# A linear-attention layer whose outputs are made feature first, with the key-value sums as weights and the denominators repeated per column

## The reference

```python
def _kernel_features(x, random_matrix):
    x_proj = jnp.einsum('bhsd,dm->bhsm', x, random_matrix)
    return (jax.nn.elu(x_proj) + 1.0) * INV_SQRT_M
...
q_prime = _kernel_features(q, random_matrix)      # 16 heads x 32 features
k_prime = _kernel_features(k, random_matrix)
kv = jnp.einsum('bhsm,bhsd->bhmd', k_prime, v)    # 32 x 8 per head
k_sum = k_prime.sum(axis=2)
out = jnp.einsum('bhsm,bhmd->bhsd', q_prime, kv)
normalizer = jnp.einsum('bhsm,bhm->bhs', q_prime, k_sum)[..., None]
normalizer = jnp.maximum(normalizer, 1e-06)
out = out / normalizer
out = out.transpose(0, 2, 1, 3).reshape(B, S, D)
return out @ Wo + bo
```

## Time and profile before

| | |
|---|---|
| median of three runs | 478.55 us (477.23 to 478.70) |
| the profiled execution | 478.46 us |
| its span, first to last instruction | 476.4 us |
| PE busy | 440.1 us, 92% |
| DVE busy | 374.5 us, 79% |
| ACT busy | 233.6 us, 49% |
| POOL busy | 104.9 us, 22% |
| granted TensorE clock, mean | 0.982 of 2.4 GHz |

### The profile page before, as it was taken

The page is one execution under the profiler, slowest core; times in us unless marked ns, Lnnn a source line. Parts: engine busy times, 40 slices in busy tenths (PEclk is TensorE's granted clock), DMA queues, the critical chain, the costliest instruction groups (busy, mean ns, idle before and its releaser), DMA issues. The chain is left out here.

```text
span 476.4 us, 8304 instructions
## 1 busy us (share of the span) xinstructions
PE 440.1 (92%) x3049; PEld 223.3 (47%) x3085; DVE 374.5 (79%) x1000; ACT 233.6 (49%) x324; POOL 104.9 (22%) x103
## 2 busy tenths in 40 slices
PE   8789979999999999999799999998999999998783
PEld 3333323333432334333243456665766675675772
DVE  6299887889689888987986298869786897887466
ACT  2405646666676665675468612336335623634220
POOL 9891070800637000200002000210020022003012
PEclk9999989999999999999999999999999999999788
DMA  5765433122432024331003222321122112000001
GB/s 160 247 172 200 101 97 112 56 78 75 123 119 96 19 72 122 113 116 31 1 24 77 35 69 88 83 72 46 45 76 59 45 37 95 3 1 23 1 1 44
DMA packets 24867, 36.19 MB, mean 76 GB/s; under 512 B 2678, under 2 KB 16246, under 8 KB 24822
## 3 DMA queue, kind: packets, MB, share of 16 engines
q1 hardware_dynamic: 24828, 35.67, 25.8%
HBM read 23.94 MB, written 11.53 MB: 74 GB/s over the span
## 5 line engine op out<-in xcount | busy, mean ns | idle before, releaser
L1156 DVE TENSOR_REDUCE negmax<-psum 128x1 f32<-128x512 f32 x256 | 169.8, 688 | 36.5 <-PE psum L541 36.3
L854 ACT ACTIVATE probs<-psum 128x1024 f32<-128x1024 f32 x128 | 127.6, 1023 | 61.2 <-PE psum L557 55.2
L541 PE MATMUL psum<-KS,QS 125*128 125x512 bf16 x256 | 98.9, 387 | 8.3 <-DVE negmax L1156 4.7
L576 PE MATMUL psum<-probs,VA 128*32 128x256 f32 x1024 | 81.0, 392 | 0.4 <-ACT probs L854 0.4
L557 PE MATMUL psum<-QS,KS 128*128 128x512 bf16 x226 | 69.9, 382 | 2.4 <-ACT probs L854 0.4
L833 PE MATMUL psum<-xT,late 128*128 128x512 f32 x144 | 68.5, 598 | 1.4 <-DVE QS L1325 1.4
L541 PEld LDWEIGHTS psum<-KS,QS 125*128 125x128 bf16 x256 | 24.6, 96 | 82.7 <-DVE negmax L1156 38.5
L463 POOL TENSOR_SCALAR var<-mv 128x4 f32<-128x4 f32 x16 | 3.6, 227 | 246.2 <-DVE mv L1063 246.1
L986 ACT ACTIVATE QS<-psum 128x512 f32<-128x512 f32 x36 | 21.6, 599 | 50.6 <-PE psum L833 50.6
L820 PEld LDWEIGHTS psum<-late,QS 128*128 128x128 f32 x288 | 35.7, 191 | 14.2 <-issue 10.8
L1325 DVE SCALAR_TENSOR_TENSOR QS<-QS,psum 128x512 f32<-128x512 f32 x36 | 24.5, 679 | 20.9 <-ACT QS L986 20.9
(11 more groups left out here) (146 smaller groups left out, 546.9 us busy)
## 6 DMA issues: line engine op xcount, KB each, us to landing
stack_dram<-parts SPq DMA_DIRECT2D x24, 384.0 KB, 3.6
cw<-w_dram SPq DMA_DIRECT2D x32, 256.0 KB, 3.2
KS<-stack_dram SPq DMA_DIRECT2D x16, 288.0 KB
QS<-stack_dram SPq DMA_DIRECT2D x16, 288.0 KB
late<-in_late SPq DMA_DIRECT2D x6, 330.5 KB, 4.6
res<-in_x SPq DMA_DIRECT2D x4, 256.0 KB, 3.6
w_dram<-wT SPq DMA_DIRECT2D x4, 256.0 KB, 4.3
out_y<-KS SPq DMA_DIRECT2D x4, 256.0 KB, 2.4
```

Source lines behind the costliest of these rows:

```text
L541: mm(sm_bank(u)[:, :], QS[b % 2][0:KROW, h, qt * P:(qt + 1) * P], KS[b % 2][0:KROW, h, :], start=True, stop=True).then_inc(sm_full, 1)
L576: last_ = mm(ps[6][32 * j:32 * j + 32, q], VA[b % 2][:, kt, h, :], probs[:, n % 2, j, q], start=(kt == 0 and half == 0), stop=(kt == NT - ...
L854: fn(probs[:, n % 2, 2 * hf:2 * hf + 2, :], psum[:, 2 * hf:2 * hf + 2, :], ACT.Exp, scale=float(DH) ** -0.5).then_inc(exp_done, 1)
L1156: V.tensor_reduce(out=negmax[:, G % 4, i:i + 1], in_=sm_bank(u)[:, :], axis=X, op=ALU.max, negate=True).then_inc(sm_free, 1)
```

## The change

The outputs are computed transposed: features on the partitions, tokens along the row. `KVB` is now two sets of weights for each group, 128 features by 32 columns: set 0 the masked key-value sums as before, set 1 the masked key sums, repeated over the 8 columns of each head. Step `O` 0 multiplies set 1 with all 512 tokens' query features, `O` 1 set 0; each is four matmuls, and group c writes PSUM partitions 32c to 32c+31. So one bank holds every output's denominator, the other its numerator. DVE sets the floor over the full 128x512 into `inv` (the memory of `attn[:, 1]`), takes four reciprocals of 128x128 in place, and multiplies by the numerators straight into `attnT`. The step `AT`, its transposes and ACT's copy are gone. The reciprocals and the product are the new generator `divided`, put at the head of `urgent`; `step(4)` takes the four reciprocals at once and leaves the product to the next call.

```diff
@@ the table of steps (in layer2 and tail_bank likewise) @@
-                 (8, "Q", 3), (8, "KT", 0), (9, "O", 0), (9, "O", 1), (10, "AT", 0), (11, "Y1", 0), (12, "norm2", 0),
+                 (8, "Q", 3), (8, "KT", 0), (9, "O", 0), (9, "O", 1), (11, "Y1", 0), (12, "norm2", 0),
...
-        KVB = sb("KVB", [P, NG, OW])
+        KVB = sb("KVB", [P, 2, NG, HW])
+        inv = attn[:, 1, :, :].rearrange("p n d -> p (n d)")
...
                 if kind == "O":
-
-                    for t in range(2):
-                        for c in range(NG):
-                            last_ = mm(cols(NG * t + c, OW), QF[:, b % 2, c, (2 * m + t) * P:(2 * m + t + 1) * P], KVB[:, c, :],
-                                       start=True, stop=True)
+                    for c in range(NG):
+                        last_ = mm(o[HW * c:HW * (c + 1), :], KVB[:, 1 - m, c, :], QF[:, b % 2, c, :],
+                                   start=True, stop=True, tile_position=(0, HW * c), skip_group_check=True)
...
-                if kind in ("attnT", "AT"):
+                if kind == "attnT":
                     for t in range(NT):
                         last_ = tr(cols(t), attn[:, b % 2, t, :], ident)
...
+            def divided(a, u):
+                dve.wait_ge(floor_done, a + 1)
+                for t in range(NT):
+                    ins = V.reciprocal(inv[:, t * P:(t + 1) * P], inv[:, t * P:(t + 1) * P])
+                    if t < NT - 1:
+                        yield
+                yield from after(ins)
+                wait_full(dve, ("Y1", a - 1, 0) if a else ("proj", last, 0))
+                tt(attnT[:, :], inv, bank_of(u)[:, :], ALU.mult).then_inc(attnT_done, 1)
+                yield
...
-                    tt(KVB[:, :, HW:OW], kv[:, :, 2 * DH:KVW].to_broadcast([P, NG, HG]), own[:, :, 0:HW:DH], ALU.mult)
-                    tt(KVB[:, :, 0:HW].rearrange("p c (r k) -> p c r k", r=2),
+                    tt(KVB[:, 1, :, :], own, kv[:, :, 2 * DH:KVW].to_broadcast([P, NG, HW]), ALU.mult)
+                    tt(KVB[:, 0, :, :].rearrange("p c (r k) -> p c r k", r=2),
...
                 if kind == "O":
                     wait_full(dve, u)
-                    if a >= 2 and m == 0:
-                        wait_full(dve, ("AT", a - 2, 0))
-
-                    v = bank_of(u)[:, 0:2 * NG * OW].rearrange("p (g k) -> p g k", k=OW)
-                    floor, inv = (rt[:, i, 32 * m:32 * (m + 1)].rearrange("p (g h) -> p g h", h=HG) for i in (20, 21))
-                    link(V.tensor_scalar(floor, v[:, :, HW:OW], 256e-6, None, ALU.max))
-                    link(V.reciprocal(inv, floor))
-                    tt(attn[:, a % 2, 2 * m:2 * m + 2, :].rearrange("p t (c h d) -> p (t c) h d", h=HG, d=DH),
-                       v[:, :, 0:HW].rearrange("p g (h d) -> p g h d", d=DH),
-                       inv.unsqueeze(3).to_broadcast([P, 2 * NG, HG, DH]), ALU.mult).then_inc(attn_done, 1)
+                    if m == 0:
+                        wait_full(dve, ("attnT", last, 0))
+                        V.tensor_scalar(inv, bank_of(u)[:, :], 256e-6, None, ALU.max).then_inc(floor_done, 1)
+                    else:
+                        urgent.insert(0, divided(a, u))
                     step(4)
```

More of the change, by code:

```diff
@@ L29 @@
 KVW = 2 * DH + 1
-OW = HW + HG
 LN_EPS = 1e-5
@@ L156, in program @@
             sem(n) for n in ("qT_done", "kT_done", "expq_done", "qf_done", "expk_done", "kf_done", "vk_done", "kvb_done"))
+        floor_done = sem("floor_done")
         kvt_done, lh_done, lsub_done, lexp_done, gh_done, ghT_done, stored = (
@@ L234, in program @@
                   ("Y2", 3, 0), ("flush", 3, 3), ("root", 3, 3), ("scale", 2, 3), ("scale", 3, 3)]
-        tail_bank = {("O", 2): 6, ("x2T", 3): 4, ("AT", 2): 5, ("kp", 3): 6, ("Y1", 2): 7, ("qp", 3): 4, ("V", 3): 5,
-                     ("KV", 3): 4, ("KT", 3): 5, ("O", 3): 0, ("x3T", 2): 4, ("lg", 2): 5, ("la", 2): 6, ("AT", 3): 7,
+        tail_bank = {("O", 2): 6, ("x2T", 3): 4, ("kp", 3): 6, ("Y1", 2): 7, ("qp", 3): 4, ("V", 3): 5,
+                     ("KV", 3): 4, ("KT", 3): 5, ("O", 3): 0, ("x3T", 2): 4, ("lg", 2): 5, ("la", 2): 6,
                      ("Y1", 3): 2, ("ghT", 2): 3, ("x3T", 3): 4, ("base", 2): 5, ("lg", 3): 6, ("la", 3): 7, ("base", 3): 0,
@@ L250, in program @@
             uses[5].append(("y_e", b, 0))
-        rotating = ("kp", "qp", "K", "Q", "V", "KV", "KT", "O", "AT", "Y1", "x3T", "lg", "la", "ghT", "Y2")
+        rotating = ("kp", "qp", "K", "Q", "V", "KV", "KT", "O", "Y1", "x3T", "lg", "la", "ghT", "Y2")
         swap = 0
@@ L289, in read_out @@
                     "Q": (expq_done, 4 * b + c + 1), "K": (expk_done, 4 * b + c + 1),
-                    "V": (vk_done, b + 1), "KV": (kvt_done, b + 1), "KT": (kvb_done, b + 1), "O": (attn_done, NB * NT + 2 * b + c + 1),
-                    "AT": (attnT_done, NB + b + 1), "Y1": (sum_done[2], b + 1), "x3T": (x3T_done, b + 1),
+                    "V": (vk_done, b + 1), "KV": (kvt_done, b + 1), "KT": (kvb_done, b + 1), "O": (attnT_done, NB + b + 1) if c else (floor_done, b + 1),
+                    "Y1": (sum_done[2], b + 1), "x3T": (x3T_done, b + 1),
                     "lg": (lsub_done, b + 1), "la": (lh_done, b + 1), "ghT": (ghT_done, b + 1),
@@ L624, in beside_pe @@
                     pe.wait_ge(attn_done, NT * (b + 1))
-                if kind == "AT":
-                    pe.wait_ge(attn_done, NB * NT + 2 * (b + 1))
                 if kind == "proj":
@@ L882, in beside_act @@
                     fn(kvt[:, :], bank_of(u)[:, 0:P], ACT.Copy).then_inc(kvt_done, 1)
-                if kind in ("attnT", "AT"):
+                if kind == "attnT":
                     wait_full(act, u)
[L885 to L889, removed]
+                    if a:
                         wait_full(act, ("proj", a - 1, 0))
```

## The result

The changed kernel takes 487.98 us, the median of four runs (487.29 to 488.28); the kernel before took 478.62 us beside it. The ratio is 1.0195, with a 95% interval of 1.0166 to 1.0224: 9.4 us slower, where 6 was forecast. The direction held. The time lies in the range that was to hold 8 in 10 (480.5 to 489), but above the forecast's own range of 483 to 487 and inside that of the rival "long falls" (487 to 490), which had a chance of 0.16. Times in this document are medians over a kernel's executions, while ratios and their intervals come from its fast executions alone.

What follows compares the result with a forecast made beforehand. The prediction took PE's waits for DVE, by instruction order, to bound the kernel. On 478.46 us it added 1.5 + 2.7 + 1.9 - 2.5 + 2.4 = +6.0, giving 484.5 us; own range 483 to 487, 8-in-10 range 480.5 to 489.

Steps and rivals of the forecast that it cites:

- long falls: Rival, chance 0.16: the clock falls at both stalls and again around block 2, staying low; 2 to 5 us more, 487 to 490.
- DVE stands in front of PE, though its busy share says it has room.: All blocks: DVE, 79% busy, gains 3.1 us a block, and PE waits for what stands behind that work.
- the three waits named: PE waits for DVE's gated product, 3.7 us in block 0, 4.9 in block 1; block 2's Y1 waits 2 for attnT.
- Block 0: +1.5.: Expert stage: DVE's gated product 2.1 us late, PE's slack 0.6 us, so PE's gate product 1.5 us late.
- Block 1: +2.7.: Expert stage: DVE's gated product 3.0 us late, PE's slack 0.3 us, so 2.7 us lost.
- Block 2: +1.9.: Tail: reciprocals stand behind the normalisation, so Y1 starts at 434.5 instead of 432.56, delaying the chain 1.9 us.
- Block 3: -2.5.: Tail: the long path itself gets shorter, Y1 2.9 us earlier, less if matmuls run at half clock; taken as -2.5 us.
- Clock: +2.4.: PE's stalls in blocks 0 and 1 bring falls to half clock, 1.2 us a stall, 2.4 us in all.
- The four column groups run together.: Output matmuls: 16 pieces of 512 columns take about 1.9 us a block; rival, groups in turn, 6.9 us, chance 0.04.

## Why the prediction was right, and which step failed

- *DVE stands in front of PE, though its busy share says it has room.* Right. Leaving the reciprocals out made the marks of blocks 0 and 1 shorter than before, and the three waits named were found, each shorter than reckoned: 2.89 us for 3.7, 4.22 for 4.9, and 1.30 for 2 at Y1 of block 2.
- *Block 0: +1.5.* Measured +1.1 (gate product 347.60 less 345.69, less the 0.8 gathered before). Reciprocals took 3.37 us instead of 3.55.
- *Block 1: +2.7.* Measured +2.4 the same way (395.37 less 389.36, less 3.6 that the block came later). The mark without half clock is +3.0. In the whole change with fillers some 0.4 of that is lost later in the block, where the transposes of the next rows start 2.14 us behind a gate product instead of 1.72, PE waiting 0.25 us for DVE's z sum. In the changed kernel that distance is 1.72 as before (400.66 to 402.38), so there the spell of half clock hides it.
- *Block 2: +1.9.* Measured +1.8 (Y1 9.59 us later where KVB was 7.80 later).
- *Block 3: -2.5.* Measured -2.75, right in size. But it is a half-clock gain; at full clock it is nothing. I had priced it at full clock as -2.9: I shortened PE's side and forgot that at full clock the old pieces and transposes would be shorter too.
- *Clock: +2.4.* This is the step that was mis-sized. Measured in the marks: 2.78 - 1.1 in block 0, 4.21 - 2.4 in block 1, 3.99 - 1.8 in block 2, together 5.7 us. The stalls of blocks 0 and 1 cost 1.7 and 1.8, where I had 1.2 each: I thought that part of a spell would lie inside the stall, but in this execution the clock fell only as PE took up work again (it is 1.00 from 390 to 395, and PE starts at 395.37), and dense products ran at half speed for all of it. Against the marks of the whole change with fillers it is 1.7, 1.2 and, less the fillers' own 1.7, 2.3, together 5.2, still over twice the 2.4. And there were three spells. Block 2's stood under "long falls", as a rival; it belonged into the sum, since PE stood there for 2.7 us (its outputs done sooner) before it stood 1.3 us for `attnT`.
- *The four column groups run together.* Right: 1.92 us for 16 pieces of 512 columns.

The forecast was 3.4 us short of the 9.4. The clock term alone was 3.3 short, but that the two numbers agree is luck: the waits and block 3 together came out 1.1 us better than forecast (0.4, 0.3, 0.1 and 0.3), and the 0.8 us that had gathered ahead of block 0, with 0.3 of difference between time and span, made up for it. What came true as a whole is the rival "long falls".

## What to carry to other kernels

Price an operation that moves to an engine by what is queued behind it on that engine at that place, not by the engine's busy share: at full clock the mark without the 3.4 us of reciprocals is shorter by 2.4 us in block 0 (40.57 for 42.96), by 3.4 in block 1 (42.65 for 46.07) and by 2.1 in block 3 (5.82 for 7.89), and only in block 3 did the new way save as much elsewhere (7.86 the old way). Where PE stands for some us amid dense work, count the clock beside the stall: here stands of 2.7 to 4.2 us were followed by spells that cost 1.7 to 2.4 us more. When work is taken off an engine that waits at that place anyhow, ask what the idle time does to its clock; filler matmuls there, with the new outputs in block 3 alone, gave the fastest kernel of this study that still computes the layer, 474.3 us, 1.2% below the kernel before; the fillers alone gave 0.5%.

## What the runs showed of the hardware

- A DVE reciprocal in fp32 grows almost in step with its width: 353, 553 and 909 ns for 32, 64 and 128 elements, where a product of 128 elements takes 285.
- PE that is busy the whole time with 36-column matmuls can still drop to half clock: 3.50 us busy of 3.50, then 0.50. It did so in one profiled execution and not in others with the same instructions at that place. That this is part of why the kernel before spreads over 7 us (476.86 to 483.87) is likely, since its time goes with its half clock, but none of its longer executions was profiled.
- Four column groups with weights from all 128 partitions start 7 ns apart in the trace, with different moving operands, and the four together take what one takes: 16 pieces of 512 columns 1.92 us, where four pieces on the whole array take 1.88.
- The clock can also fall while PE stands idle: in one execution it was 0.50 for the last 2 us of a stand of 4.22 us, in another with the same stand 1.00 until PE had taken up work again.
